# Shift products on 64-row halves, another static order, and three feed-forward stages in one block

## The reference

```python
x1  = layernorm(x  + self_attention(x, alibi_bias))          # 16 heads of 16
x2  = layernorm(x1 + cross_attention(x1, ctx))               # softmax over the 112 query rows, axis=1 of (n, l, h, s)
xq  = act_qdq(x2)                                            # 16-bit integers, one scale for the whole tensor
gate, up = xq @ Wg.T, xq @ Wu.T                              # weights dequantised from 4-bit blocks, 768 x 256
gate, up = act_qdq(gate), act_qdq(up)
glu = act_qdq(gate * fixed_qdq_u16(sigmoid(gate)))
h   = act_qdq(glu * up)
out = layernorm(x2 + h @ Wd.T)
```

## Time and profile before

| | |
|---|---|
| median of 3 runs | 1333.27 us (1332.06 to 1335.41) |
| the profiled execution | 1335.2 us, of which its span is 1333.4 us |
| TensorE (PE) busy | 1201.2 us, 90% of the span |
| VectorE (DVE) busy | 1110.1 us, 83% |
| ScalarE (ACT) busy | 872.4 us, 65% |
| GpSimd (POOL) busy | 344.9 us, 26% |
| mean granted TensorE clock | 0.96 |

### The profile page before, as it was taken

The page is one execution under the profiler, slowest core; times in us unless marked ns, Lnnn a source line. Parts: engine busy times, 40 slices in busy tenths (PEclk is TensorE's granted clock), DMA queues, the critical chain, the costliest instruction groups (busy, mean ns, idle before and its releaser), DMA issues. The chain is left out here.

```text
span 1333.4 us, 27769 instructions
## 1 busy us (share of the span) xinstructions
PE 1201.2 (90%) x8850; PEld 901.2 (68%) x8850; DVE 1110.1 (83%) x2358; ACT 872.4 (65%) x2290; POOL 344.9 (26%) x431
## 2 busy tenths in 40 slices
PE   1689999999999999999999999999867868859598
PEld 1467766777776777766777766776536757659598
DVE  6269999999999999999999999999863448958698
ACT  1466766766767766766766767666423459959695
POOL 0223343233343233343233342322300000000043
PEclk9999999999999999999999999999968979979799
DMA  5100000100000000000000000000000000000033
GB/s 162 34 27 17 20 20 27 31 19 18 18 18 24 31 18 18 18 18 25 30 18 18 18 18 27 29 20 5 5 8 4 0 0 1 0 0 0 18 104 100
DMA packets 35042, 33.07 MB, mean 25 GB/s; under 512 B 4148, under 2 KB 34604, under 8 KB 34988
## 3 DMA queue, kind: packets, MB, share of 16 engines
q1 hardware_dynamic: 32704, 31.50, 7.8%
q10 hardware_dynamic: 2284, 0.89, 0.3%
HBM read 25.04 MB, written 7.34 MB: 24 GB/s over the span
## 5 line engine op out<-in xcount | busy, mean ns | idle before, releaser
L564 ACT ACTIVATE Px<-score 125x896 f32<-125x896 f32 x192 | 176.4, 919 | 186.8 <-PE score L1081 116.0
L732 DVE TENSOR_REDUCE Zc<-Px 125x8 f32<-125x896 f32 x192 | 207.2, 1079 | 32.6 <-ACT Px L564 32.6
L750 DVE TENSOR_REDUCE nmax_c<-score 125x8 f32<-125x896 f32 x192 | 206.1, 1073 | 2.1 <-PE score L1003 1.8
L557 ACT ACTIVATE Ps<-score,nmax_s 112x112 f32<-112x112 f32 x512 | 173.6, 381 | 5.7 <-DVE nmax_s L757 5.7
L1081 PE MATMUL score<-sel,nmaxT 128*125 128x448 f32 x384 | 126.4, 410 | 1.9 <-ACT nmaxT L570 1.9
L486 POOL TENSOR_TENSOR Kbd_hi<-Ks_hi,mask 128x448 fp32r<-128x448 f32 x64 | 63.9, 999 | 229.5 <-DVE Ks_lo L766 229.5
L507 POOL TENSOR_TENSOR rstd<-vare,half 112x1 f32<-112x1 f32 x64 | 35.0, 546 | 332.5 <-DVE vare L842 332.5
L557 ACT ACTIVATION_READ_ACCUMULATOR Ps<-score,nmax_s 112x1 f32 x512 | 120.2, 235 | 0.0
L1092 PE MATMUL outX<-Px,Vn 125*32 125x224 f32 x1536 | 106.4, 365 | 2.3 <-DVE Vn L743 2.2
L1003 PE MATMUL score<-Qbd_hi,KxT_hi 64*125 64x448 f32 x384 | 90.9, 470 | 3.6 <-ACT Px L564 2.8
L570 ACT ACTIVATE nmaxT<-maxT 128x125 fp32r<-128x125 f32 x192 | 53.5, 279 | 51.9 <-PE maxT L1075 51.7
(11 more groups left out here) (245 smaller groups left out, 3541.2 us busy)
## 6 DMA issues: line engine op xcount, KB each, us to landing
ctx_in<-in_ctx SPq DMA_DIRECT2D x32, 375.0 KB
x_in<-in_x SPq DMA_DIRECT2D x32, 112.0 KB, 2.1
x_scratch<-x SPq DMA_DIRECT2D x32, 112.0 KB, 1.9
x2T_all<-x_scratch SPq DMA_DIRECT2D x32, 112.0 KB, 2.1
out<-x2T_all SPq DMA_DIRECT2D x32, 112.0 KB, 1.9
raw_w_up<-in_w_up SPq DMA_DIRECT2D x1, 768.0 KB, 5.5
raw_w_down<-in_w_down SPq DMA_DIRECT2D x1, 768.0 KB, 7.4
raw_w_gate<-in_w_gate SPq DMA_DIRECT2D x1, 768.0 KB, 9.5
```

Source lines behind the costliest of these rows:

```text
L557: ins = act.activation(Ps[:, g, :], score[slot][0:L, h // QUAD, (h % QUAD) * L:(h % QUAD + 1) * L], ACT.Exp, bias=nmax_s[:, g:g + 1], accu ...
L564: act.activation(Px[u % 2][:].rearrange("s (q h) l -> s q (h l)", q=2), score[SLOT_OF[f"C{u}"]][0:C, :, 0:QW], ACT.Exp).then_inc(exp_c, 1)
L732: dve.tensor_reduce(Zc[p][:], Px[p][:], AX.X, ALU.add).then_inc(z_c, 1)
L750: dve.tensor_reduce(nmax_c[u % 2][:, 0:OCT].rearrange("s (q h) -> s q h", q=2), score[SLOT_OF[f"C{u}"]][0:C, :, 0:QW].rearrange("s q (h l) ...
```

## The change

It has three parts.

1. `shift` becomes one pair of 64-row matmuls. `max_cross` writes the maxima of the heads of bank q=0 to columns 0 to 3 and those of q=1 to columns 64 to 67 of `nmax_c`, so that after the transpose they stand in rows 0 to 3 and 64 to 67 of `nmaxT`. `sel` shrinks to 448 columns and holds the same four selector rows in both row halves (two small loads in place of one).
2. Every engine's `step` in `attention` gets another order, with other batch indices, and `WORK_USES` and `SLOT_USES` go with it. On TensorE the last six calls become the first six of the next step, and the shifts of units 1, 2, 3, 5 and 0 come to stand directly behind `self_scores` or `cross_scores`. `norm_cross` gets a wait for `xmax_done`.
3. `gate_product`, `gated` and `hidden_values` become one block, `gate_and_up`. TensorE goes from one stage's products into the next one's, with the global maxima's products in between. The gate's maxima go by halves. ScalarE makes the x parts of the next group between the two halves of its step, and those of the next stage's first group in the last step. The turning of `w_down` is spread: two fills at the seam, two in the first group of up. A sigmoid on one column is issued at the seam.

```diff
-        sel = sb("sel", [P, OCT * L], F32R)
+        sel = sb("sel", [P, QW], F32R)
...
+            def of_halves(t):
+                return t[:].rearrange("s (q x) -> s q x", q=2)[:, :, 0:QUAD]
...
-                dve.tensor_reduce(nmax_c[u % 2][:, 0:OCT].rearrange("s (q h) -> s q h", q=2),
+                dve.tensor_reduce(of_halves(nmax_c[u % 2]),
...
                 for q in range(2):
-                    ins = pe.matmul(score[SLOT_OF[f"C{u}"]][0:C, q, 0:QW], nmaxT[u % 2][:, 0:C],
-                                    sel[:, q * QW:(q + 1) * QW], start=False, stop=True, skip_group_check=True)
+                    rows = slice(HALF_ROWS * q, HALF_ROWS * (q + 1))
+                    ins = pe.matmul(score[SLOT_OF[f"C{u}"]][0:C, q, 0:QW], nmaxT[u % 2][rows, 0:C], sel[rows],
+                                    start=False, stop=True, skip_group_check=True)
```

The steps of the new block that the prediction speaks of, on ScalarE first:

```diff
+            def gate_step(g, p, last):
+                store_gate(g, 0)
+                if last:
+                    parts(UP, 0, 0)
+                else:
+                    act.wait_ge(xpart_done, g + 2)
+                    parts(GATE, g + 1, 1 - p)
+                store_gate(g, 1)
...
+            def hidden_step(g, p, last):
+                first = isinstance(g, int) and g == 0
+                up_integers(g, 0)
+                if first:
+                    up_integers(g, 1)
+                    act.wait_ge(scales_ready, 1)
+                glu_integers(g, 0)
                 if not last:
+                    parts(HIDDEN, g + 1, 1 - p)
+                if not first:
+                    up_integers(g, 1)
+                glu_integers(g, 1)
```

On VectorE:

```diff
+            def up_step(g, p, last):
+                largest_up(g, 0)
+                glu(g, 0)
+                if isinstance(g, int) and g == 0:
+                    down_low(2)
+                    down_low(3)
+                else:
+                    largest_glu(g - 1, 1)
+                largest_up(g, 1)
+                if last:
+                    dve.wait_ge(up_maxed, NH)
+                    top["up"].spread_out(dve, maxima["up"][:])
+                    largest_glu(g, 0)
+                    top["up"].gather(dve)
+                    small.quantiser(top["up"].top, tiny["x_scale"], tiny["up_scale"], tiny["up_inv"])
+                    dve.tensor_copy(tiny["up_unit"][:], tiny["up_scale"][:]).then_inc(up_ready, 1)
+                    glu(g, 1)
```

On TensorE:

```diff
+            def up_step(g, p, last):
+                products(UP, w_up, g, p, 0, up_maxed, gate_stored)
+                if isinstance(g, int) and g == 0:
+                    pe.wait_ge(lo_done, 2)
+                    top["gate"].tensor(pe)
+                    turn_down(2)
+                    pe.wait_ge(top["gate"].top_done, 1)
+                    turn_down(3)
+                products(UP, w_up, g, p, 1, up_maxed, gate_stored)
+
+            def hidden_step(g, p, last):
+                products(HIDDEN, w_up, g, p, 0, up_q_done, up_maxed)
+                if isinstance(g, int) and g == 0:
+                    top["up"].tensor(pe)
+                products(HIDDEN, w_up, g, p, 1, up_q_done, up_maxed)
+                if isinstance(g, int) and g == 0:
+                    top["glu"].tensor(pe)
```

More of the change, by code:

```diff
@@ L1411, in _ @@
-            small.done(dve.tensor_scalar(tiny["x_scale"][:], top[0].top[:], 1.0 / QMAX, TINY, ALU.mult, ALU.max))
-            small.done(dve.reciprocal(tiny["x_inv"][:], tiny["x_scale"][:]))
-            quantise_x(0)
-            over_groups(dve, step)
-            dve.wait_ge(maxed, NG)
-            top[1].vector(dve, maxima[:])
-            small.quantiser(top[1].top, tiny["x_scale"], tiny["gate_scale"], tiny["gate_inv"])
-        @block.tensor
-        def _(pe):
-            pe.wait_ge(ones_done, 1)
-            top[0].tensor(pe)
-            over_groups(pe, lambda g, p, last: products(pe, w_gate, xh, bank, g, p, x_parts, product, stored))
-            top[1].tensor(pe)
@@ L1516, in _ @@
+            down_low(1)
+            top["gate"].gather(dve)
+            small.quantiser(top["gate"].top, tiny["x_scale"], tiny["gate_scale"], tiny["gate_inv"])
+            dve.tensor_scalar(tiny["glu_unit"][:], tiny["gate_scale"][:], 1.0 / SIGQ, None, ALU.mult)\
+                .then_inc(gate_ready, 1)
+            over_groups(dve, up_step)
             largest_glu(NG - 1, 1)
```

719 lines of the change are left out of this document (358 added, 361 removed).

## The result

The changed kernel takes 1314.64 us (median of 4 runs, 1313.49 to 1314.99) against 1333.95 of the kernel before beside it (1332.06 to 1335.41): a ratio of 0.986 (0.984 to 0.987), 19.3 us saved. The forecast was 1287 us, 46.5 us saved, with a range up to 1308: the time lies above it. The profiled execution has a span of 1311.7 us against 1333.4, which is 21.7 less.

What follows compares the result with a forecast made beforehand. TensorE was taken to bound attention, serial hand-overs the feed-forward half. Savings of 31 + 8.9 + 6.4 + 0.2 = 46.5 us gave 1287 us; own range 1278 to 1298, 8 in 10 within 1272 to 1308.

Steps and rivals of the forecast that it cites:

- gate to up: Seam from gate stage to up stage: shorter seam saves 8.0 us, longer up stage costs 1.6; 6.4 us saved.
- up to hidden: Seam and hidden stage: joined block's gain taken back by later x parts, 5.4 us over six groups; 0.2 us saved.
- part 2: Attention's new static order: 27.5 us a batch, 1.0 less with the halved shifts; 31 us over 31 periods, bounds 12 and 43.
- Part 1: Attention's shift as a 64-row pair: 1.23 us of TensorE time saved per batch, about 0.2 us of seams against it.
- rival (c): Attention's shift halves run in a row, not overlapped; seams cost 0.2 us; 1324 us, chance 0.04.
- Rival (d): Attention's four new seams cost full 0.2 us each, nothing given back; 0.43 us a batch saved, 1305 us, chance 0.10.
- Rival (a): VectorE takes over as attention's bound; 28.1 us a batch, 1306 us, chance 0.17.
- Rival (b): All small waits of both engines in attention go too; 27.1 us a batch, 1275 us, chance 0.12.
- Fill, drain and the seam into the gate stage: Before the first and behind the last attention batch: fill and drain, same chain, costed at nothing, +-3 us.
- Parts 3 to 5: Feed-forward half: gate stage 8.9 us saved, gate to up 6.4, up to hidden 0.2; 15.5 us together.
- T: Up stage: the end of the last but one sigmoid piece, 1166.39 in the kernel before.
- rival (f): Clock does not fall at up to hidden; 2.9 us more, inside the range; no chance of its own given.

Runs made afterwards that it cites:

- spare reductions: Changed kernel, straight-line iterations only: two reductions with unused results on VectorE ahead of the normalisation of unit 4, so it is issued later; 1328.71 us.
- the row at 168.45: From the changed kernel with GpSimd's root of kind 1 moved behind `diagonal_keys(.., 1)`: normalisation issued at 168.45 within a product, waited for that one only; 1295.48 us.
- gap run: Changed kernel; in straight-line iterations GpSimd waits, behind its root of kind 1, for that root's own semaphore before the products; 1282.44 us, 0.961 of before.
- with full rows: Changed kernel with the shift back on two 128-row products and the old places of the maxima, new order and joined block kept; 1355.72 us, 1.016 of before.
- With halves: Kernel before with part 1 alone, the shift as one pair of 64-row products in the old order; 1315.05 us, 0.987 of before.
- The early parts: Changed kernel with ScalarE's x parts of the next group first in the hidden step, group 1's ahead of the wait for up's scale; 1301.5 us, 0.976.

## Why the prediction was wrong

**The steps against the profile.** Saved, in the profiled executions:

| | forecast | measured |
|---|---|---|
| attention | 31 | 6.7 (880.82 to 874.16) |
| seam to the gate stage | 0 | -1.7 |
| gate stage | 8.9 | 10.3 |
| gate to up | 6.4 | 7.3 |
| up to hidden | 0.2 | -0.5 |
| tail | 0 | -0.4 |
| sum | 46.5 | 21.7 |

**The step that failed** is the one in part 2 on GpSimd: "its share is 68.90 of 200, so I cost these at nothing". A share tells whether an engine has time. It doesn't tell what the engine does to another one beside it. The root was moved directly ahead of the four products, and VectorE's normalisation is issued behind it. In its place the runs showed five holds of 4.03 to 4.20 us, each 5.6 to 6.5 us of period with the clock, 30.4 us in all. In the kernel before, no products stood behind a root of kind 1, and VectorE's longest wait for GpSimd there was under 1 us (a normalisation of 1.02 us, 0.26 without). The Trainium skill has a rule for such meetings in "SBUF — State Buffer", section "Who interferes with whom": a VectorE instruction with two SBUF inputs contends with a GpSimd instruction that reads SBUF, and the second to issue blocks until the first has finished. The normalisation has two such inputs, the spare reductions one, and these were not held (0.73 us for two, beside the power and the first product). By that rule each meeting costs at most the rest of one product, 0.9 us, which the row at 168.45 bears out. The 4.03 us are beyond it: here the measurement decides. The gap run shows the term whole: without the hold attention takes 842.7 us, 31.5 less than in the kernel after and 38.1 less than before, where 31 was forecast, and the time is 1282.4, 4.6 under the forecast. So the rest of the reasoning erred the other way: by 7.1 us in attention, by less in the sum.

**Part 1.** Right in kind: pairs overlap, so rival (c) is out. Its net price was put at 1.03 us a batch, seams of the new order included, and 1.31 were measured in the new order: a shift behind scores has no near seam any more. In the old order it is 0.87 of TensorE's work. Rival (d) takes the rule of the Trainium skill's page "TensorEngine Tiling (Array Packing)", Key Properties, that a switch of the tiling mode drains TensorE, and prices it by the rows at 0.2 us for each of four new seams. It would have 28.1 us a batch; the loop has 27.39. The new order has the four seams more, and with full rows it takes 0.36 us more of TensorE's work (28.34 to 28.70): about 0.09 us each, the price that the forecast gave.

**Part 2, period.** 27.5 forecast, 27.39 measured. The order alone gains nothing: with full rows the period goes from 28.53 to 28.70. With halves it goes from 27.94 to 27.39, nearly all of it TensorE's waits: 0.47 us a batch go, and its work falls from 27.47 to 27.39. Rival (a) is out: VectorE has 190.56 of 200, 26.1 us a batch, and TensorE doesn't wait. Rival (b) was near in its mechanism, as no wait is left, yet not in its 27.1. Waits of VectorE after, 300 to 700 us, which answer to the earlier trace rows: those for the exponential fell from 12.4 us to 2.4, those for scores went from 5.8 to 8.4.

```profile
DVE nmax_c L755 <- PE score L1011: 8.4, 15, 0.6
...
DVE Zc L734 <- ACT Px L564: 2.4, 14, 0.2
```

**Fill, drain and the seam into the gate stage** were put at nothing, +-3 us. In the gap run the last two periods take 25.5 and 21.8 us in place of 27.1 and 26.9, 6.7 us less, of which the forecast had 2. After them, up to the gate's first products, 0.3 us are lost in that run (31.49 us against 31.19; 32.90 in the kernel after). So the two brought 4.4 us more than forecast. The other 2.4 us of attention are the loop's: 27.39 for 27.5 over 22 batches. Ahead of the first batch that trace has 2.4 us more than before (98.19 against 95.83); over the fifteen traces this stretch varies from 95.8 to 98.8 us, and why was not looked into.

**Parts 3 to 5.** Order of time of the kernel after, ScalarE and TensorE, which answers to the earlier trace rows:

```profile
1032.11 0.94 ACT L1397 ACTIVATE xq_hi<-x2T_all 128x896 fp32r x1
...
1039.31 0.94 ACT L1397 ACTIVATE xq_hi<-x2T_all 128x896 fp32r x1
...
1063.23 1.29 ACT L1402 ACTIVATE U<-gbank 128x1344 f32<-128x1344 f32 x1 [0.63 <-PE gbank L1606]
...
1069.54 1.42 ACT L1420 ACTIVATE up_q<-U,gate_inv 128x1344 int16<-128x1344 f32 x1 [2.74 <-DVE glu_unit L1571]
...
1143.83 0.93 ACT L1397 ACTIVATE xq_hi<-x2T_all 128x896 fp32r<-128x896 int16 x1
...
1221.23 1.38 ACT L1446 ACTIVATE up_q<-gbank,up_inv 128x1344 int16<-128x1344 f32 x1 [0.91 <-PE gbank L1606]
...
1160.72 0.74 PE L1604 MATMUL gbank<-xq_hi,w_upT_hi 128*128 128x448 f32 x1 [4.64 <-ACT xq_lo L1398]
...
1171.20 0.47 PE L1604 MATMUL gbank<-xq_hi,w_upT_hi 128*128 128x448 f32 x1 [0.93 <-ACT xq_lo L1398]
```

A gate group takes 7.20 us (forecast 7.44). From the gate's last product to the first sigmoid piece there are 6.31 us (forecast 6.8), from there to T, now 1143.83, 74.3 (74.7), and from T to the last product of hidden 77.4 (76.7). TensorE idles 4.64 us at the seam (5 to 7), its clock falls as forecast (0.83 from 1150 to 1170), so rival (f) is out, and it waits 0.93 us for the x parts in a group (0.9). A group takes 8.5 us (near 8.3). The early parts confirm that the late ones have a price, and show it too low: 13.1 us, where 5.4 was given to the groups and nothing to the seam, which had been put down to the maxima alone. Over five groups they give back 7.7 us of it, and the clock at the seam up to 3.4 (0.17 of 20 us).

**The chances.** 0.95 for faster was right. None of the rivals was this one: the search for what a moved instruction can harm went through waits and queues, and left out what GpSimd's instructions do to VectorE's while both run. With the wait behind the root the time is 1282 us, inside the range of the forecast.

## What to carry to other kernels

When an instruction of GpSimd is moved, look at which VectorE instructions with two SBUF inputs start while it and the row behind it run, not at GpSimd's share. Where a power on GpSimd is followed directly by long instructions and VectorE has such an instruction to issue, put a wait for the power's own semaphore behind it: here that was enough, and it moved nothing. And read the straight-line iterations of a pipeline apart from its loop: the same order of calls gives other code there, and a mean over the loop hides them.

## What the runs showed of the hardware

- Behind a power of 112x1 on GpSimd (0.55 us), products of 128x448 that follow directly kept a VectorE instruction with two inputs in SBUF out until the last of them ended: 4.03 us with four products, 3.38 when it was issued 0.65 us later, 2.25 with two. Behind a product in the power's place, or in a row whose power stands further back, it waited for one product and took 0.58 to 1.16 us in all. Single-input reductions were not held.
- A wait for the power's own semaphore, or the loop's register instructions, between the power and the products ends this, though in the loop the products start no later (0.51 us behind the root's start in both). Waits that the products carry for semaphores raised long before do not end it.
- Issued 64 to 66 ns behind the power's start, the same instruction was held in three traces (4.20 us); issued 63 ns behind it, it was not in two (0.29 us).
- A TensorE wait of 3.0 us within otherwise full work was followed by about 7 us at the lower clock level, so that the price of the wait doubled: 6.3 us a batch.
